# Position-bias tables of a Swin block: gathered with the tables as weights, laid out through memory

## The reference

```
bias = rel_table[rel_index]                 # table (169, 6), index (49, 49) -> (49, 49, 6)
attn = einsum('bhnd,bhmd->bhnm', q, k) + bias.transpose(2, 0, 1)
if shifted: attn += mask                    # one of four kinds of window
attn = softmax(attn)
```

## Time and profile before

| | us |
|---|---|
| median of 3 runs (7252.24 to 7257.74) | 7252.71 |
| the profiled execution, its own time | 7256.51 |
| its span, first to last instruction | 7254.8 |
| stage 1, to the last copy of `cm` | 0 to 172.3 |
| masks, index and first one-hot matrices | 172.3 to 178.3 |
| gathering and layout of the three tables | 178.3 to 416.5 |
| folding of weights, clearing of V, first loads | 416.5 to 443 |
| main loop and end | 443 to 7254.8 |

### The profile page before, as it was taken

The page is one execution under the profiler, slowest core; times in us unless marked ns, Lnnn a source line. Parts: engine busy times, 40 slices in busy tenths (PEclk is TensorE's granted clock), DMA queues, the critical chain, the costliest instruction groups (busy, mean ns, idle before and its releaser), DMA issues.

```text
span 7254.8 us, 329797 instructions
## 1 busy us (share of the span) xinstructions
PE 7012.4 (97%) x144058; PEld 5013.7 (69%) x144058; DVE 3317.7 (46%) x6706; ACT 4465.9 (62%) x6913; POOL 2235.0 (31%) x2070
## 2 busy tenths in 40 slices
PE   6879999999999999999999999999999999999997
PEld 4867776777677777776777677777777677677764
DVE  6144444444444444444444444444444444444444
ACT  0026666666666666666666666666666666666660
POOL 4013333333333333333333333333333333333330
PEclk9999999999999999999999999999999999999995
DMA  8000000000000000000000000000000000000007
GB/s 247 5 13 24 22 25 23 24 23 24 23 24 24 23 24 23 24 23 24 23 24 22 24 23 24 23 24 23 23 24 23 25 23 24 23 24 22 24 18 233
DMA packets 287573, 243.59 MB, mean 34 GB/s; under 512 B 42174, under 2 KB 281760, under 8 KB 285856
## 3 DMA queue, kind: packets, MB, share of 16 engines
q1 hardware_dynamic: 241506, 179.61, 9.2%
q10 hardware_dynamic: 36414, 19.95, 0.9%
q0 software_dynamic: 8192, 22.49, 0.9%
HBM read 112.73 MB, written 109.18 MB: 31 GB/s over the span
## 4 chain that ended last, share of the span: by engine, by line
PE 94%; DMA 3%; issue 2%; DVE 1%; ACT 0%; POOL 0%; SPq 0%; POOLq 0%; DVEq 0%; ACTq 0%
PE pS L934 14%; PE pA L976 13%; PE pS L947 9%; PE pA L897 7%; PE pB L985 6%; PE pS L956 5%; PE pB L1033 5%; PE pA L1025 5%; PE pB L1016 4%; PE pB L1054 4%; PE pB L1073 4%; PE pA L903 4%; PE pA L1064 3%; PE pB L993 3%; PE pB L1081 3%; PE pA L993 2%
## 5 line engine op out<-in xcount | busy, mean ns | idle before, releaser
L442 POOL TENSOR_TENSOR Kbd<-KT,headmask 128x588 f32<-128x588 f32 x768 | 896.9, 1168 | 3468.5 <-DVE KT L719 3468.5
L708 DVE TENSOR_REDUCE mx<-pS 113x12 f32<-113x588 f32 x1536 | 1180.8, 769 | 1258.6 <-PE pS L956 1252.9
L934 PE MATMUL pS<-bias,stackr 128*128 128x296 f32 x6096 | 1332.9, 341 | 3.0 <-ACT E L502 2.7
L502 ACT ACTIVATE E<-pS 113x588 f32<-113x588 f32 x1536 | 1005.7, 655 | 450.7 <-DVE mx L708 421.3
L442 POOL TENSOR_TENSOR Qbd<-Qt,headmask 128x588 f32<-128x588 f32 x768 | 897.1, 1168 | 1062.6 <-DVE Qt L713 1062.6
L934 PEld LDWEIGHTS pS<-bias,stackr 128*128 128x128 f32 x6096 | 931.4, 189 | 327.0 <-issue 226.0
L486 ACT ACTIVATE sq<-pB 112x392 f32<-112x392 f32 x768 | 382.0, 497 | 1076.6 <-PE pB L985 1076.6
L976 PEld LDWEIGHTS pA<-E,V 113*54 113x54 f32 x36864 | 957.4, 130 | 110.8 <-issue 110.6
L976 PE MATMUL pA<-E,V 113*54 113x49 f32 x36864 | 1005.6, 214 | 0.9 <-ACT va L491 0.8
L947 PE MATMUL pS<-Kbd,Qt 24*49 24x147 f32 x24576 | 765.7, 304 | 0.3 <-issue 0.3
L956 PE MATMUL pS<-Qbd,KT 27*49 27x147 f32 x24576 | 706.8, 285 | 0.0
(11 more groups left out here) (126 smaller groups left out, 9694.2 us busy)
## 6 DMA issues: line engine op xcount, KB each, us to landing
xin<-xT SPq DMA_DIRECT2D x384, 98.0 KB, 2.0
xT<-xout SPq DMA_DIRECT2D x384, 98.0 KB, 1.9
xin<-xT SPq DMA_DIRECT2D x384, 73.5 KB, 2.0
xT<-xout SPq DMA_DIRECT2D x384, 73.5 KB, 1.8
xT<-cm POOLq DMA_DIRECT2D x128, 171.5 KB, 3.6
cm<-xT SPq DMA_DIRECT2D x128, 171.5 KB, 3.3
tm<-in_x SPq DMA_DIRECT2D x128, 147.0 KB
out<-tm ACTq DMA_DIRECT2D x128, 147.0 KB
```

The costliest lines, as they stand in the source:

```text
L442: return pool.tensor_tensor(y, x, m, ALU.mult)
L502: act.activation(e, s, ACT.Exp).then_inc(exp_done, 1)
L708: dve.tensor_reduce(m, s, AX.X, ALU.max).then_inc(mx_done, 1)
L934: mm(pS[:, q, S1:S1 + 2 * SW], stackr[:, :], rows, start=True, stop=False)
```

## The change

The two operands of the gather change places. The table's columns are the weights (6 of table 0, 12 of tables 1 and 2 together), and the one-hot matrix streams past them, up to 490 columns at a time (`PART`: 10, 10, 10, 10 and 9 groups of 49). For each entry of TABLES that is 2 ways x 5 parts x 2 (lo, hi) = 20 products, 40 in all. For the first way the stream is contiguous, for the second it steps by 49 elements. The result lies by head: 6 or 12 partitions x 2401. ScalarE copies each part from PSUM to the new tile `gath`, in a ring of four banks. SyncE writes `gath` to the new tensor `gat` in memory, waits for it, and reads it back into `whole` with eight transfers for each table (way x partition half x half of the heads), each 49 partitions x 3 heads x 49 numbers. VectorE's four copies per table are gone; it waits for the transfers (`whole_in`), and counts `whole_used` up when it is done with `whole`, for which SyncE waits before it refills it.

```diff
--- before.py
+++ after.py
@@ -106,6 +106,7 @@
 
         scratch = [nc.dram_tensor(f"xT{k}", (PAIRS, R, IMG), fp32, kind="Internal").ap()
                    for k in range(NPH + 1)]
+        gat = nc.dram_tensor("gat", (2, 2 * HEADS, 2, N * N), fp32, kind="Internal").ap()
         x_tm = A["x"].rearrange("(P i) h w c -> P i (h w c)", i=2)\
                      .rearrange("P i (g p e) -> P g p i e", g=G, p=TP)
         o_tm = out.rearrange("(P i) h w c -> P i (h w c)", i=2)\
@@ -155,7 +156,8 @@
             idx_f = tmp("idx_f", [128, N * N])
             oh_lo = tmp("oh_lo", [128, N * N])
             oh_hi = tmp("oh_hi", [128, N * N])
-            tab = tmp("tab", [128, NPH, 2, HEADS])
+            tab = tmp("tab", [128, 2, NPH * HEADS])
+            gath = tmp("gath", [32 + 2 * HEADS, 2, N * N])
             neg = tmp("neg", [M2, NPH, 3, N])
             whole = tmp("whole", [128, 2, 4, 2, SW])
             high = tmp("high", [128, 2, 4, 2, SW], fp32r)
@@ -203,7 +205,8 @@
         par_in = sem("par_in")
         idx_in = sem("idx_in")
         onehot = sem("onehot")
-        tab_mm = sem("tab_mm")
+        gat_mm, gat_done, gat_out = sem("gat_mm"), sem("gat_done"), sem("gat_out")
+        whole_in, whole_used = sem("whole_in"), sem("whole_used")
         set_up = sem("set_up")
         bias_mm = sem("bias_mm")
         scaled = sem("scaled")
@@ -266,13 +269,14 @@
                 par += col(t, j, A[v])
             for k, j in enumerate((BQ, BK, BV)):
                 par += headcol(t, j, bqkv, k * C)
-            par.append((tab[:, t, 0, :], A[ph["table"]][0:128, :]))
-            par.append((tab[0:REL - 128, t, 1, :], A[ph["table"]][128:REL, :]))
+            par.append((tab[:, 0, HEADS * t:HEADS * (t + 1)], A[ph["table"]][0:128, :]))
+            par.append((tab[0:REL - 128, 1, HEADS * t:HEADS * (t + 1)], A[ph["table"]][128:REL, :]))
         consts = [(ident[:, :], A["ident"]), (center[:, :], A["center"]), (ones[:, :], A["ones"]),
                   (headmask[:, :], A["headmask"]), (minus[:, :], A["minus"]), (kcol[:, :], A["kcol"]),
                   (stack[:, :], A["stack"]), (select[:, :], A["select"]), (spread[:, :], A["spread"]),
                   (regions[0:N, :, :], A["regions"]), (regions[HI:M2, :, :], A["regions"])]
         TABLES = [("rel_const", [0]), (L1 + "rel_index", [1, 2])]
+        PART = [(10 * c, min(10, N - 10 * c)) for c in range(5)]
         CLEARED = [tz, wq, wk, wv, wvr, wvh, wp, w1, w2ab, w2c, cols, b1c, tab, whole, neg, Qbd, mx]
 
         def flat(tile):
@@ -366,6 +370,21 @@
                     load_x(Step(u, c))
             sp.wait_ge(onehot, 1)
             load_index(1)
+            for k, (_, ts_) in enumerate(TABLES):
+                n = len(ts_) * HEADS
+                sp.wait_ge(gat_done, 10 * (k + 1))
+                sp.dma_start(gat[k, 0:n], gath[32 * k:32 * k + n]).then_inc(gat_out, 16)
+                sp.wait_ge(gat_out, 16 * (k + 1))
+                for t in ts_:
+                    if t:
+                        sp.wait_ge(whole_used, t)
+                    for way in range(2):
+                        for r in (0, HI):
+                            for hh in range(2):
+                                h = HEADS * (t - ts_[0]) + HP * hh
+                                sp.dma_start(whole[r:r + N, way, 0, hh, 0:WN].rearrange("p (h m) -> p h m", m=N),
+                                             gat[k, h:h + HP, way].rearrange("h (n m) -> n h m", m=N))\
+                                  .then_inc(whole_in, 16)
             for b in range(4):
                 sp.wait_ge(cm_out[b], 16 * STEPS // 4)
             sp.wait_ge(set_up, 1)
@@ -480,6 +499,16 @@
                 act.dma_start(to, of).then_inc(par_in, 16)
 
             act.preload_act_table_set("natural_log_exp_and_others")
+
+            g = 0
+            for k, (_, ts_) in enumerate(TABLES):
+                rows = slice(32 * k, 32 * k + len(ts_) * HEADS)
+                for way in range(2):
+                    for a, n in PART:
+                        act.wait_ge(gat_mm, g + 1)
+                        act.activation(gath[rows, way, N * a:N * (a + n)], bank[2 + g % 4][rows, 0:N * n], ACT.Copy)\
+                           .then_inc(gat_done, 1)
+                        g += 1
 
             def square(j, mm, src, dst, done):
                 act.wait_ge(mm, gv(j, 1, 1))
@@ -618,26 +647,18 @@
                 for r in (0, HI):
                     chain(dve.tensor_scalar(neg[r:r + N, t], regions[r:r + N], ph["neg"], None, ALU.mult))
 
-            def heads(ap):
-
-                return strided(ap, [[SW, 2], [N, HP], [1, N]])
-
-            tables = 0
             for k, (_, ts_) in enumerate(TABLES):
                 dve.wait_ge(idx_in, 16 * (k + 1))
                 chain(dve.tensor_copy(idx_f[:, :], idx_i[:, :]))
                 if k:
-                    dve.wait_ge(tab_mm, 1)
+                    dve.wait_ge(gat_mm, 10)
                 dve.tensor_scalar(oh_lo[:, :], idx_f[:, :], kcol[:, 0:1], None, ALU.is_equal)
                 dve.tensor_scalar(oh_hi[:, :], idx_f[:, :], kcol[:, 1:2], None, ALU.is_equal).then_inc(onehot, 1)
                 for t in ts_:
-                    tables += 1
-                    dve.wait_ge(tab_mm, tables)
+                    dve.wait_ge(whole_in, 128 * (t + 1))
                     kinds = 4 if PH[t]["shift"] else 1
                     for way in range(2):
                         for r in (0, HI):
-                            src = strided(bank[3 * way + t][r:r + N, 0:1], [[HP, 2], [1, HP], [HEADS, N]])
-                            chain(dve.tensor_copy(heads(whole[r:r + N, way, 0, 0, 0:1]), src))
                             for kind in range(1, kinds):
                                 for hh in range(2):
                                     last = dve.tensor_tensor(
@@ -657,7 +678,7 @@
                                 last = dve.tensor_tensor(bias[HI:128, at, :, way, :], whole[HI:128, way, kind, :, :],
                                                          high[HI:128, way, kind, :, :], ALU.subtract)
                     chain(last)
-
+                    dve.sem_inc(whole_used, 1)
 
             chain(dve.memset(pA[:, :, :], 0.0))
             dve.wait_ge(bias_mm, NPH)
@@ -855,18 +876,22 @@
 
             pe.wait_ge(par_in, 16 * len(par))
 
+            g = 0
             for k, (_, ts_) in enumerate(TABLES):
                 pe.wait_ge(onehot, k + 1)
-                for t in ts_:
-                    for way in range(2):
-                        for r in (0, HI):
-                            for m in range(N):
-                                o = bank[3 * way + t][r:r + N, HEADS * m:HEADS * (m + 1)]
-                                at, by = ((m, N), (m * N, 1))[way]
-                                mm(o, strided(oh_lo[:, at:at + 1], [[by, N]]), tab[:, t, 0], start=True, stop=False)
-                                last = mm(o, strided(oh_hi[:, at:at + 1], [[by, N]]), tab[:, t, 1],
-                                          start=False, stop=True)
-                    last.then_inc(tab_mm, 1)
+                c = HEADS * ts_[0]
+                heads = slice(c, c + len(ts_) * HEADS)
+                rows = slice(32 * k, 32 * k + len(ts_) * HEADS)
+                for way in range(2):
+                    for a, n in PART:
+                        if g >= 4:
+                            pe.wait_ge(gat_done, g - 3)
+                        at, by = ((a * N, [[1, N * n]]), (a, [[1, n], [N, N]]))[way]
+                        o = bank[2 + g % 4][rows, 0:N * n]
+                        mm(o, tab[:, 0, heads], strided(oh_lo[:, at:at + 1], by), start=True, stop=False)
+                        mm(o, tab[:, 1, heads], strided(oh_hi[:, at:at + 1], by), start=False, stop=True)\
+                            .then_inc(gat_mm, 1)
+                        g += 1
             for t in range(NPH):
                 o = 8 * t
                 be1, be2 = cols[0:C, t, BE1:BE1 + 1], cols[0:C, t, BE2:BE2 + 1]
```

## The result

| | before | after |
|---|---|---|
| first comparison, median of 4 runs each, us | 7255.23 | 7146.92 |
| ratio, 95% interval | | 0.9847 [0.9835, 0.9859] |
| second comparison (7 and 4 runs), us | 7257.28 | 7135.87, ratio 0.9835 [0.9818, 0.9851] |
| profiled execution, its span, us | 7256.51, 7254.8 | 7153.04, 7151.3 |

A forecast was written before the change was run, and what follows sets the result against it. The bound was the table stage's relay between TensorE and VectorE: its terms summed to 108.5 us instead of 238.3, a gain of 129.8, giving 7126.7 by the profiled execution or 7122.9 by the median; forecast 7125, range 7110 to 7158.

The forecast's parts named there:

- Where the time is: Table stage: TensorE and VectorE take turns in a 238.3 us chain, so each microsecond saved there shortens the whole program.
- wrong in kind: Sign of failure: VectorE's three waits together exceed 190 us, or the 6.6 ms main loop moves by more than 10 us.
- The stream and its price: New gather on TensorE: 0.85 ns a column-record at 2.4 GHz, 16.3 us for an entry of TABLES.
- The step of 49: Second way's stream of the one-hot matrix in the gather: no cost taken; bound 8 us an entry.
- The clock: Each burst of gather products starts 4.8 us at the low clock, then rises; 2.4 us more, 18.7 us an entry.
- The rival of a clock that stays low: Low clock through both entries' gather on TensorE: 27.8 us more, 7153 us; chance 22%.
- The trip: Gathered table through memory: write 3.0 us, a table's eight reads 7.3 us, of which 1.6 us beyond issue and landing.
- Slow pieces: Rival: each table's 196-byte read pieces over only four engines at 41.6 ns, 10.6 us more, three times: 7158; chance 11%.
- the rival of one engine: A table's read pieces pass through one DMA engine, 48.9 us, 44.1 more than reckoned, three times: 7257; chance 2%.
- seven engines: Skill's rule for reads of 49 partitions: 168 pieces on each engine, sum up to 3 x 3.3 = 10 us longer.
- The main loop I leave as it is: Main loop taken as unchanged, starting from the same idle TensorE; only some 5 us allowed for code lying elsewhere in memory.
- The forecast's own range: Whole program without the rivals: 7112 with faster reads, no low start and code placement, to 7140 with slower steps; chance 62%.

The follow-up runs named there:

- e5_overlap: e3_one_stream with VectorE's one-hot matrices made ahead of the loop over tables, two buffers of whole and an arrival semaphore for each; 7078.17 us, ratio to before 0.9756.
- e1_both_contiguous: The changed kernel with both ways streaming the one-hot matrix contiguously, so its output is not the program's; median 7127.18 us.
- e2: The changed kernel with the way that steps by 49 first in each burst and the contiguous way second; one run, 7145.07 us.
- e7_um24: The changed kernel with a main-loop body of 24 steps instead of 40, 15 passes instead of 9; 7172.38 us.
- e0_after: The changed kernel itself, unaltered, timed again beside the kernel before; 7135.87 us, ratio 0.9835.
- e3_one_stream: The changed kernel streaming only the contiguous way, ScalarE writing each part twice, straight and with a step of 49; 7100.80 us, ratio to before 0.9791.
- e6_nops: The changed kernel with 200 empty TensorE instructions ahead of its wait for scaled, so later code lies elsewhere; 7140.17 us.
- e9_two_queues: e5_overlap with half of each table's reads issued on ScalarE's queue, behind its copies; 7072.95 us, ratio to before 0.9752.

## Why the prediction came out as it did

*Where the time is.* Right: the relay of the earlier trace rows was the path, each piece of it fell or grew as an item of its own, and e5_overlap shows the reverse, that pieces taken off the relay cost nothing. VectorE's three waits came to 78.8 us, far from the 190 that would have meant wrong in kind.

*The stream and its price.* Right for the contiguous way: 0.82 us a product at the high clock, 490 x 2 records x 0.85 = 0.83 reckoned.

*The step of 49.* This is the step that failed: "I take no cost". It costs 0.92 us a product, 9 us an entry, 18 in all (e1_both_contiguous: 18.1); the bound in the same sentence, twice the time for half the stream, 8 us an entry, was passed by 1. The row it rested on the earlier trace rows could not decide: those weight loads, by the prediction's own reading, ran at the low clock, and e2 shows that there a stepped read (1.74) and a straight one (1.6) are hardly apart.

*The clock.* Right: low for the first 4.85 us of the first burst (181.68 to 186.53) and about 4.7 of the second, 4.8 reckoned. That it came out to the tenth is luck. By the same reckoning (1.63 us a product at the low pace, 0.82 at the high) the low start of the first burst was 3.3 us in e7_um24, 4.35 in e0_after and 5.7 in e3_one_stream, whose products begin alike. The rival of a clock that stays low is out; the clock rose in every burst, with 6 weight columns in the first and 12 in the second. The column of the granted clock reads 1.00 at 181 us, where the products say low, and 0.50 from 210.4 on: before its first change it can't be trusted.

*ScalarE.* Right: 0.57 us a copy (0.576), one showing at the end.

*The trip.* Two wrong sizes that cancelled in part: 9.3 us for 11.1. The write took 4.13 us from issue to the first read's issue (209.93 to 214.06), 3.0 reckoned. What was mis-sized is the row, 1.0 us by the index load. The write's packets, from 209 to 214 us:

```profile
DMA packets 12, 0.12 MB, mean 23 GB/s; under 512 B 6, under 2 KB 6, under 8 KB 6
q1 hardware_dynamic: 12, 0.12, 17.3%
```

17.3% of 16 x 5 us is 13.8 us for six rows, 2.3 us each. Each row of 19.2 KB is one packet: the packed trace has the first from 210.70 to 213.41 us and the last until 213.69; two took 1.5 us, four 2.6 to 2.8. (A table of stretches books a packet's whole time where the packet starts, so it shows the DMA engines idle from 211.5 us on, when these rows were still moving.) The reads took 4.6 instead of 7.3: issue 3.02 us for eight (3.7 reckoned), landing sooner, no time for the pieces beyond it. A piece took 17 ns, between the 11.3 and the 41.6 of the earlier trace rows. Slow pieces are out, and so is the rival of one engine, which needed 49 us a table. The two rivals were not reckoned alike: four engines were counted as if their pieces began after the issue, one engine as if they ran beside it. By the second way four engines would have given 7.4 us more a table instead of 10.6, some 7148 instead of 7158. Likewise the 3.3 us a table added for seven engines leave out the 1.6 us that the term already had.

*VectorE.* Right: 16.94, 4.36, 3.00, 16.95 against 17.0, 4.35, 3.2, 17.0.

*The sum.* 108.5 reckoned, 119.8 found: bursts +17.8, trips with handover -3.5, table 2's reads -2.7, the rest -0.3. With this the working gives 7134 (by the median) to 7138 (by the profiled execution) instead of 7123 to 7127, and the second comparison gave 7135.87. The first gave 7147. In its profile the relay started 3.4 us later (181.68 for 178.3), and from the first product of the main loop to the first transpose back it took 6680.6 us, 12.7 more than before; e0_after took 6667.0 there, e3 6659.2, e1 and e2 some 6682.5. The prediction put the main loop at nothing ("The main loop I leave as it is") but for 5 us on code placement, which no row showed, and named a loop that moves by more than 10 us as a sign of being wrong in kind. The first profile crossed that line with 12.7, e0_after did not (0.9 less than before). So this is a second step that failed, in the first comparison at least.

The shortfall of the granted clock, added up over the whole loop and not only behind the turns, accounts for nearly all of it:

| | loop, us | shortfall in it, us | loop less shortfall, us |
|---|---|---|---|
| after, first profile | 6680.6 | 61.8 | 6618.8 |
| e0_after | 6667.0 | 46.5 | 6620.5 |
| e1_both_contiguous | 6682.6 | 66.2 | 6616.4 |
| e2_strided_way_first | 6682.3 | 66.1 | 6616.3 |
| e3_one_stream | 6659.2 | 42.6 | 6616.6 |
| e5_overlap | 6665.4 | 49.1 | 6616.3 |
| e6_nops | 6664.1 | 41.6 | 6622.5 |
| e7_um24 | 6704.8 | 65.3 | 6639.5 |
| e9_two_queues | 6659.6 | 42.8 | 6616.8 |

The loops differ by 23 us among the eight executions with a body of 40 steps, and the last column by 6; e7_um24 stands 19 to 20 above e0_after there, its longer waits. 18 to 29 us of the shortfall lie in the first 150 us of the loop, which starts from a TensorE that stood idle, 10 to 29 behind the turns and 8 to 15 in the drain. In the profile before, the column's first change comes only at 490.8 us, 57 us into the loop; if that start is taken as low, as the earlier trace rows says, 6617.6 is left there too. So the loop's own work stayed the same within some 6 us, and its length goes with the low clock at its start and behind its turns, in a share that changes from one execution to the next. The shift of the code in e6 had no effect. What decides when the clock rises, and whether it falls at a given turn, was not tried and stays open.

*The range.* It held both medians, but not for the reason it was drawn for. The forecast's own range ended at 7140, and the rest up to 7158 was there for a clock that stays low in the bursts, which did not happen. The first median (7146.92) lies in that rest, brought there by the step of 49 (11 us net of what the reads gave back) and the main loop (some 13): that part is luck.

## What to carry to other kernels

Where engines take turns, price a change piece by piece against the stage's own relay; a share over the whole span says nothing about it. When operands change places, look at both new access patterns at the clock at which they will run. Let an engine with spare time (here ScalarE, on its writes) take the awkward stride: in this stage one stream with two copies was worth 32 us of stage on top of the change. Then ask which piece still has to wait for another: reordering and a second buffer gave 28 more.

## What the runs showed of the hardware that I had not expected

- An fp32 stream read with a step of 49 elements takes 1.78 ns for each column of a record (1.74 us / 980) at either clock; a straight one 0.84 at the high and 1.66 at the low clock. A stepped write costs ScalarE 1.01 us instead of 0.57 for 490 columns.
- A write of 112.5 KB to memory from 6 partitions is six packets of 19.2 KB, of 1.5 to 2.8 us each, that begin 0.8 us after the issue; the waiting queue goes on 4.1 us after the issue. The 225 KB from 12 partitions, twelve packets side by side, took the same (268.09 to 272.28).
- A wait of 2.67 us at a loop's turn was followed by some 17 us of TensorE at half speed, and waits of the same kind at other turns by none; a step of 0.001 in the mean granted clock is about 6 us of this program (e3: 24 us over 0.004).
